# Cross-attention and expert kernel: the next head's loads issued from ACT's queue, one block per period, and the projections' places moved

## The reference

```python
x = x + _L0_xattn_ref(ctx_1024, _layernorm(x), ...)        # attention with 16 heads
x = x + _L0_ffn_ref(_layernorm(x), ...)                    # experts
x = x + _L1_xattn_ref(_layernorm(x), ctx_1024, ...)        # second cross attention
x = x + _L1_ffn_ref(_layernorm(x), ...)                    # experts
# in _L0_xattn_ref; x is the context there, the latents are the tokens:
q = lat @ Wq                                               # 1024 x 1024
kv = jnp.concatenate([x, lat], axis=1) @ Wkv               # 7428 keys, K and V
dots = jnp.einsum('bhid,bhjd->bhij', q, k) * scale         # per head 1024 x 7428, 64 deep
attn = jax.nn.softmax(dots, axis=-1)
out = jnp.einsum('bhij,bhjd->bhid', attn, v)
```

## Time and profile before

| what | us |
|---|---|
| median of 3 runs | 2502.02 (2498.89 to 2502.21) |
| the profiled execution | 2494.57 |
| its span | 2492.8 |
| PE busy | 2303.6 |
| DVE busy | 1864.0 |
| POOL busy | 1846.9 |
| ACT busy | 1673.9 |

### The profile page before, as it was taken

The page is one execution under the profiler, slowest core; times in us unless marked ns, Lnnn a source line. Parts: engine busy times, 40 slices in busy tenths (PEclk is TensorE's granted clock), DMA queues, the critical chain, the costliest instruction groups (busy, mean ns, idle before and its releaser), DMA issues. The chain is left out here.

```text
span 2492.8 us, 68127 instructions
## 1 busy us (share of the span) xinstructions
PE 2303.6 (92%) x27961; PEld 1491.0 (60%) x27961; DVE 1864.0 (75%) x2822; ACT 1673.9 (67%) x3037; POOL 1846.9 (74%) x1105
## 2 busy tenths in 40 slices
PE   2999999999999999999999999999999998689987
PEld 1365665566566655665666556655666556558875
DVE  8877777887787878877877787878777761467754
ACT  4677777777677777776777677767777776246642
POOL 1798888989888988898889888888889998120000
PEclk9899999999999999999999999999999999889988
DMA  2612223132413141414131413141313000600000
GB/s 87 164 40 57 72 79 99 49 83 67 111 38 96 56 122 36 97 56 122 36 93 60 118 40 94 61 117 40 93 61 88 2 2 10 186 10 2 2 4 9
DMA packets 107639, 165.57 MB, mean 66 GB/s; under 512 B 23544, under 2 KB 97216, under 8 KB 102208
## 3 DMA queue, kind: packets, MB, share of 16 engines
q1 hardware_dynamic: 104032, 157.12, 23.0%
q10 hardware_dynamic: 3296, 4.10, 0.5%
HBM read 99.22 MB, written 61.97 MB: 65 GB/s over the span
## 5 line engine op out<-in xcount | busy, mean ns | idle before, releaser
L608 POOL TENSOR_TENSOR att_prob_low<-att_prob 128x1024 f16<-128x1024 f32 x960 | 1765.5, 1865 | 230.0 <-PE all_banks L728 126.4
L885 ACT ACTIVATE att_prob<-all_banks 128x512 f32<-128x512 f32 x1888 | 1070.7, 591 | 366.3 <-PE all_banks L693 247.7
L979 DVE TENSOR_REDUCE att_part<-all_banks 128x2 f32<-128x1024 f32 x800 | 946.5, 1218 | 197.9 <-PE all_banks L653 197.9
L714 PE MATMUL all_banks<-att_v,att_prob 128*128 128x129 f16 x5664 | 584.1, 221 | 2.8 <-DVE shared_att L1003 0.6
L714 PEld LDWEIGHTS all_banks<-att_v,att_prob 128*128 128x128 bf16 x5664 | 414.6, 98 | 238.0 <-issue 10.8
L728 PEld LDWEIGHTS all_banks<-att_v,att_prob_low 128*128 128x128 f16 x7552 | 328.8, 98 | 138.4 <-POOL att_prob_low L608 18.7
L674 PE MATMUL all_banks<-att_qc,att_kc 128*128 128x512 f16 x1056 | 401.3, 380 | 0.0
L675 PE MATMUL all_banks<-att_qd,att_kd 128*128 128x512 f16 x1056 | 401.0, 380 | 0.0
L728 PE MATMUL all_banks<-att_v,att_prob_low 128*128 128x65 f16 x7552 | 386.0, 194 | 13.4 <-POOL att_prob_low L608 13.4
L718 PE MATMUL all_banks<-att_v,att_prob 128*128 128x64 f16 x1888 | 371.2, 197 | 0.0
L716 PE MATMUL all_banks<-att_v,att_prob 128*128 128x65 f16 x1888 | 365.9, 194 | 0.0
(11 more groups left out here) (304 smaller groups left out, 3074.8 us busy)
## 6 DMA issues: line engine op xcount, KB each, us to landing
att_kc<-k_high SPq DMA_DIRECT2D x30, 928.5 KB, 10.8
att_v<-v_all SPq DMA_DIRECT2D x14, 1870.5 KB
v_all<-att_stage_v SPq DMA_DIRECT2D x98, 258.0 KB, 2.4
att_kd<-k_low SPq DMA_DIRECT2D x16, 928.5 KB, 15.0
k_high<-att_stage_h SPq DMA_DIRECT2D x98, 128.0 KB, 1.7
k_low<-att_stage_l SPq DMA_DIRECT2D x98, 128.0 KB, 1.9
att_kd<-k_low SPq DMA_DIRECT2D x16, 208.0 KB, 15.7
prep_ctx<-in_ctx SPq DMA_DIRECT2D x5, 640.0 KB, 9.1
```

The costliest lines, as they stand in the source:

```text
L608: pool.tensor_tensor(prob_low[g % NL][:, 0:w], p[:, 0:w], p.bitcast(BF16)[:, 1:2 * w:2], op=ALU.subtract).then_inc(low_split, 1)
L714: pe.matmul(O[:, q, :], w, v[:, e, t, :], start=first, stop=False, skip_group_check=True)
L885: act.activation(prob[g % NP][:, i * BANK:(i + 1) * BANK], S[n % 3], ACT.Exp, scale=SCALE)\
L979: dve.tensor_reduce(parts[:, n:n + 2], pers.banks[:, 4 + 2 * pair:6 + 2 * pair, :], axis=AX.X, op=ALU.max)\
```

## The change

1. SP issues no load in the loop over heads any more. ACT does: `load_next` is called in each period behind `exp(n + 2)`. In w = 1 to 7 it issues one of the seven transfers of `load_kq` each, behind waits on `scored` and, in an odd head, on `kq_out` in w = 1. The values' two transfers go in w = 9 of an even head (not head 0) and in w = 25 of an odd one (before: 0 and 23).
2. `KQ_AT` goes from 0, 2, 4, 6, 8, 9, 10, 12, 14, 16, 18, 19, 20, 22, 24, 26, 28 to 1, 3, 5, 7, 9, 11, 12, 14, 16, 17, 19, 20, 22, 23, 25, 26, 28. `V_AT` goes from 0, 1, 3, 4, 6, 7, 9, 10, 12, 15, 16, 18, 19, 21, 22 to 1, 3, 4, 6, 7, 9, 10, 12, 14, 16, 17, 19, 20, 22, 23. So nothing is projected in periods 0 and 15, and both kinds of head project in 14.

```diff
@@ -384,8 +384,8 @@
-        KQ_AT = sorted([*range(0, PERIODS, 2), 9, 19])
-        V_AT = [w for w in range(23) if w % 3 != 2 and w != BACK_AT]
+        KQ_AT = [1, 3, 5, 7, 9, 11, 12, 14, 16, 17, 19, 20, 22, 23, 25, 26, 28]
+        V_AT = [1, 3, 4, 6, 7, 9, 10, 12, 14, 16, 17, 19, 20, 22, 23]
...
@@ -529,18 +509,6 @@
                 for w in range(PERIODS):
-                    if w == 0 and b + 1 < HEADS:
-                        if b:
-                            sp.wait_ge(scored, b * HEAD_TILES)
-                        if b and e:
-                            for r in range(NR):
-                                sp.wait_ge(kq_out[r], kq_writes(i + 2, r))
-                        if b == 0:
-                            sp.wait_ge(filled, 1)
-                        load_kq(b + 1)
-                        if b and not e:
-                            sp.wait_ge(low_done, LOW0 + b * UNITS)
-                            load_v(b + 1)
                     if projecting:
...
-                        if e and w == V_AT[-1] + 1:
-                            for r in range(NR):
-                                sp.wait_ge(v_out[r], v_writes(i + 2, r))
-                            sp.wait_ge(low_done, LOW0 + b * UNITS)
-                            load_v(b + 1)
@@ -843,6 +806,63 @@
         @block.scalar
         def _(act):
...
+            def load_kq(m, x):
+
+                e = m % 2
+                r = slice(m * DH, (m + 1) * DH)
+                if x == 0:
+                    act.dma_start(kc[0:DH, e, 0:KEYS], k_high[r, :]).then_inc(k_in[e], 16)
+                elif x == 1:
+                    act.dma_start(kc[DH:P, e, 0:KEYS], k_high[r, :]).then_inc(k_in[e], 16)
...
+            def load_next(b, e, i, w, projecting):
+
+                if b + 1 == HEADS:
+                    return
+                if w == 1:
+                    act.wait_ge(scored, b * HEAD_TILES)
+                    if b == 0:
+                        act.wait_ge(filled, 1)
+                    elif e:
+                        for r in range(NR):
+                            act.wait_ge(kq_out[r], kq_writes(i + 2, r))
+                if 1 <= w <= 7:
+                    load_kq(b + 1, w - 1)
+                if w == 9 and b and not e:
+                    act.wait_ge(low_done, LOW0 + b * UNITS)
+                    load_v(b + 1)
+                if w == V_AT[-1] + 2 and e and projecting:
+                    for r in range(NR):
+                        act.wait_ge(v_out[r], v_writes(i + 2, r))
+                    act.wait_ge(low_done, LOW0 + b * UNITS)
+                    load_v(b + 1)
@@ -897,6 +917,7 @@
                     exp(n + 2)
+                    load_next(b, e, i, w, projecting)
                     if not last:
                         exp(n + 3)
```

39 lines of the change are left out of this document (22 added, 17 removed).

## The result

The changed kernel takes 2456.86 us (median of 4, 2455.83 to 2458.05), the kernel before 2500.45 us beside it (median of 4, 2495.37 to 2502.21). The ratio is 0.9829, with a 95% interval of 0.9812 to 0.9846: faster by 1.7%, or 43.6 us between the two medians. The forecast was 2468.7 us with a range from 2460 to 2491.

A forecast was written before the change was run, and what follows sets the result against it. The prediction took PE, busy 92% of the span, to bound the kernel. Gains of 21.6 + 3.4 + 2.5 + 5.8 = 33.3 us, taken from the median of 2502.02, gave 2468.7 us, range 2460 to 2491.

The forecast's parts named there:

- The median of the runs shown lies 7.45 us above it.: Kernel before: runs' median 2502.02 us against the profiled 2494.57; this offset was added to the forecast of 2461.3 us.
- Loads leave SP's queue: Writes no longer stand behind loads in SP's queue, so ACT's 13 DMA waits go: 21.6 us gained.
- the two figures given: Bounds for the loads' move: 22.8 us excess in ACT's DMA waits, 20.5 us in PE's own waits; the middle taken.
- Key projection off period 0: Heads 2 to 12, six: saves 1.37 us at the head's end, costs 0.81 elsewhere; 3.4 us gained in all.
- Value projection off period 0: Seven odd heads, 0.36 us each: 2.5 us gained, with bounds of -5.7 and +3.9 us.
- 15 to 14: Value projection moved from period 15 to 14 in seven odd heads: 5.8 us gained, between 5.1 and 6.4.
- Head 0 at nothing: Key projection off period 0: head 0 starts otherwise than heads 2 to 12, so no gain was counted there.
- 133 issues on ACT: Loads issued between ACT's exponentials cost 0 if its queue runs ahead of the engine; upper end 12 us.
- the two starts that the prediction gave: A load's issue on ACT can begin at 383.42, or with the exponential at 384.54; both end by about 385.03.
- The writes stay late: Rival, chance 0.07: writes wait for loads wherever these are issued, so the 21.6 us stay: 2490.3 us.
- the two rows: Sign: PE's projection waits L631 and L621 behind VectorE's reduction L979 fall from 27.5 us to a few.
- the 8.8 named: Sign: the stretch across a head's end, 10.20 or 10.00 us before, comes near 8.8 us.

The follow-up runs named there:

- SP spread: The changed kernel with its loads issued by SP instead of ACT, the same blocks in the same periods: 2457.19 us, ratio 0.9841 against the kernel before.
- the last kernel with the loads on SP: The changed kernel with loads spread on SP, VectorE's addition L1030 deferred to periods 1 and 16, and the last key task in period 29, not 28: 2436.52 us.

## Why the prediction missed

The working fails at one step, is too small at one term (the value projection), and is right or near at the others. The time itself lay outside the range because of the first.

- **The step that failed: "The median of the runs shown lies 7.45 us above it."** I carried this to a kernel that doesn't have it. The miss of 11.8 us splits in three: 7.45 of this step; 0.75 more because the profiled execution of the changed kernel is above its median (2457.61 against 2456.86); and 3.66 because the sum was small (2461.27 forecast for an execution like the profiled one, 2457.61 measured). The 7.45 us had two sources. First, the median of three runs, 2502.02, was itself high: beside the experiments the kernel before took 2496.91, 2494.98, 2497.14 and 2498.08 us (9 to 14 runs each). Second, two executions of the kernel before differ by 5.7 us in their loop, 3.5 of it in the two heads where a fall of the clock follows a DMA wait. The change removes those waits, and two executions of the changed kernel differ by 0.1 us. An offset between a profile and a median belongs to what varies, and I should have asked whether the change takes that away. With offset 0 the forecast is 2461.3 us and the lower end of the range, worked out in the same way, some 2453 us, which takes in the 2456.86 measured.
- **Loads leave SP's queue, 21.6 us.** The periods that held the waits lost 22.9 us, measured as the excess of periods 4 and 5 (even heads) and 3 (odd) over the undisturbed ones. That is at the upper of the two figures given, 20.5 and 22.8, and it holds the one fall of the clock in head 2, which neither list of waits counts. The sum rests on the waits alone and came out right, but the reason was only half right. What matters isn't that the loads leave SP's queue: it is enough that they are spread, in either queue, or that the first reuse comes late enough after them. The new places alone do that on SP, so in the sum this term and the places aren't separate parts. (The prediction calls the L653 matmuls scores; they are the window's.)
- **Key projection off period 0, 3.4 us.** Measured 10.20 - 8.78 = 1.42, less 0.81, times 6: 3.7 us.
- **Value projection off period 0, 2.5 us.** Measured 10.00 - 8.60 = 1.40, less 0.71 for its new place (period 23 takes 4.28 us with it and took 3.57), times 7: 4.8 us. The nearest row, the stretch of 8.83 us into an even head, was not the same stretch: into an odd head it is 0.2 us shorter. And the price of 0.81 is that of a key projection. This term was off by nearly its own size, and lies above its upper bound of 3.9 for both reasons.
- **15 to 14, 5.8 us.** 10.00 - 9.11 = 0.89, times 7: 6.2 us.
- **Head 0 at nothing.** Head 0 became 1.24 us longer in the two traces compared. That can't be put down to the change: its first period takes 5.89 and 7.03 us in two executions of the kernel before. What differs is how long the clock stays at its lower level there: the granted clock from 122 to 126 us is 0.81 and 0.54 in these two, and 0.52 in the changed kernel, whose first period takes 6.18 us. At a like clock, 0.81, the projection's move saves 0.95 us of the period (5.89 to 4.94, the latter with only period 0 emptied) and costs its 0.81 elsewhere, so nothing was a fair term.
- **Together** 22.9 + 3.7 + 4.8 + 6.2 - 1.2 = 36.4, where the loop over heads 0 to 14 lost 36.3 us (1871.55 to 1835.21); 0.6 lie outside this loop. The -1.2 is head 0's clock, by the last point, and not the change. Profiled execution to profiled execution it is 36.96 us (2494.57 to 2457.61) against 33.3.
- **133 issues on ACT, 0.** The number is right, and of the two starts that the prediction gave, the later one is what happened: the issue begins with the exponential directly ahead, and never with the one before it. The rule cited from the Trainium skill, Perfetto Trace Analysis (the section on DVE and Act instructions), that the sequencer is free once it has pushed an instruction to the wait queue, agrees with the early end of the wait L884, but not fully with the issues. By it alone an issue could begin while the exponential ahead still waits for PE; none does (501.52 against 501.51, after a wait of 0.60 us). Nor does it make issues free: a second one in the same gap held ACT for 0.61 us.
- **"The writes stay late"**, the rival from the Trainium skill, DMA: Bandwidth & Descriptors (Issuing engines are not separate DMA queues). What the page says, that DMAs of all issuers interleave on the same engines and another issuer buys no bandwidth, agrees with the runs: SP spread and ACT spread take 2457.19 and 2456.86 us, and with all loads at once from ACT the writes in SP's queue still land up to 12.1 us after their issue. What I made of it, that late writes would stay in this kernel, doesn't follow; spreading in time moves the worst landing from 16.2 us to 9.5 or 6.2.

What each step would show came as written: no DMA wait, 2.4 us in the two rows, 8.78 and 8.60 beside the 8.8 named, 9.11 beside 9.1, value periods of 4.24 us, no issue in ACT's queue above 2 us.

## What to carry to other kernels

When a small write is late behind a burst of loads, measure from the burst's start to the next use of the buffer before moving any transfer: one period later in a table of places did what a new queue for 5 MB of loads did. In this kernel ACT could issue one DMA for nothing beside an exponential that is longer than the issue; what came on top was paid with the engine's time, because its next instruction was the one that PE waited for. And a gap between a profile and the runs' median may be carried over to a change only if what makes the gap is still there.

## What the runs showed of the hardware

- At the same instruction of head 4 a pause of PE of 1.71 us was followed by a window with a granted clock of 0.62, and a pause of 1.98 us by one of 1.00. With only period 0 emptied and the loads on SP, six pauses of 2.5 to 3.0 us had two falls behind them. So the length of the pause alone doesn't decide. Behind the longer pause of head 2 with all loads at once, the window from 392 to 396 us is at 0.50 throughout.
- A DMA issue on ACT began 0.01 us after the start of the exponential ahead of it, also where that one had waited for PE. It took 0.45 to 0.47 us for the first six blocks of a head (0.54 at most), 0.61 to 0.64 us for the seventh and 0.32 to 0.35 us for the values' first. Back to back with others it took 0.61 to 0.63 us, and behind seven others 1.78 and then 0.96 us; on SP a write's issue behind the loads took 3.32 us.
- With all loads of an even head issued at once in SP's queue, the first 128 KB write of `q_low` landed 25.1 to 25.6 us after the first load, whether it was issued 9.2 or 11.9 us after it.
- With the same bytes in the same periods, writes landed within 6.2 us when the loads were in SP's own queue and within 9.5 us when they were in ACT's. Both came again: 6.4 us in the last kernel with the loads on SP, 9.4 us in the second trace of the changed kernel. I had expected the reverse. I have no run that says why.
